# Embedding rows by indirect transfers on GpSimd in place of a one-hot product on TensorE

## The chip, the cores and the metric

The kernel runs on one core of one Trainium2 chip. The time is the device time of one execution in microseconds; the kernel before has a median of 807.42 us in 3 runs (805.93 to 807.51). The profiled execution took 805.65 us; its span, from the first to the last recorded instruction, is 803.5 us.

The engines are TensorE (PE: matmuls; PEld: its weight loads, which overlap them), VectorE (DVE), ScalarE (ACT), GpSimd (POOL) and SyncE (SP, which here issues transfers only). Each runs its own instruction list in order, and they meet through semaphores.

## The reference

Tokens of shape (2, 2048), 0 to 69, become rows of 192 numbers; then one block with a state-space mixer, a gated MLP and a routed mixture of 8 experts follows. Only the embedding is changed:

```
t = minimum(tokens, 63);  color, shape, quantity = t // 16, t % 16 // 4, t % 4
feat_emb = concatenate([color_W[color], shape_W[shape], quantity_W[quantity]])
spec_emb = special_W[clip(tokens - 64, 0, 5)]
emb = where(tokens < 64, feat_emb, spec_emb)
h = emb * sqrt(192) + position                 # (2, 2048, 192)
h = h + block(layernorm(h))                    # the mixer runs along the 2048 tokens
h = h + experts(layernorm(h))                  # 2 of 8 experts per token, and a shared one
```

The host lays the 70 possible rows out in one table (64 combinations of features and 6 special rows), so that a token is the number of its row.

## The kernel before

The 2048 tokens are cut into 16 chunks of 128 (`NC`, `Q`), and a chunk holds both sequences (`NB` = 2), so most tiles are 128 tokens by 2 x 192 numbers, or 128 channels by 256 tokens. The order of every engine's work is written out by hand. Three chunks are under way at a time: `body(p, f, b)` runs the embedding, norm and input products of chunk p, the scan of chunk f = p-1 and the MLP and experts of chunk b = p-2. `ramp` does chunks 0 and 1 up to there, `body` is run 14 times (once written out, 13 times in a loop), and `finale` does the last two chunks.

The embedding of a chunk is `pre`. Before the change it goes: SP fetches the chunk's tokens, broadcast on 70 partitions (`load`, L370), and the position rows; DVE compares them with the row numbers `ids` (`pre_onehot`, L1060), which gives a one-hot tile of 70 x 256; PE multiplies it with the table, which DVE has split into three bf16 parts at the start (`setup_table`, L1002 to L1010), in 6 matmuls (`pre_embed`, L1558); DVE adds the position rows (`pre_add`, L1067) and takes mean and variance (`pre_stats`); POOL raises the variance to the power -0.5 (`rsqrt`, L444); ACT and DVE write the normed rows as high and low halves (L812, L1052), and PE turns them (`pre_turn`, L1572) for the input products.

In a round PE embeds inside `swiglu` (L1864), the gate and up products of chunk b's MLP. These are six pairs (f = 0 to 5) of 10 matmuls on two PSUM banks `p_pair` in turn, so pair f waits until DVE has read pair f-2 (`gt_ready`, L1873; DVE writes `gt` at L1222 from ACT's `sg`, L792). `pre_embed` stands after pair 1, before pair 2. DVE has the one-hot step after `scanned(f, 0)` and `pre_add` after the second `gt` (L1229). POOL has, between `pre(p)` and `norm2(b)` (L603 to L605), nothing.

```
                    if f >= 2:
                        pe.wait_ge(gt_ready, c * NF + f - 1)
                    mlp_gate_up(c, f, p_pair[f % 2])
                    if f == 1 and p is not None:
                        pre_embed(p)
```

Of the kernel before, what the change touches and what calls it, by code (L numbers as in the profile page):

```python
# [21 lines left out]
ALU = mybir.AluOpType  # L22
# [4 lines left out]
BF16 = mybir.dt.bfloat16  # L27
I32 = mybir.dt.int32

NB = 2  # L30
# [70 lines left out]

def program(nc, tokens, position, vocab_ids, table, weights, norms, conv_w, conv_b, shared_rows, d_skip, w_out, w_down,
            w2, identity, lower_ones, triangle_rows, exponent_rows, pair_rows, spread_rows, out):
    with ExitStack() as ctx:
        def sb(name, shape, dt=F32):
            return ctx.enter_context(nc.sbuf_tensor(name, shape, dt))

        def sem(name):
            return ctx.enter_context(nc.semaphore(name))


        ids = sb("ids", [V, 1])
        tab = sb("tab", [V, D])
        tab_rest = sb("tab_rest", [V, 2, D])
        tab3 = sb("tab3", [V, 3, D], BF16)
        w_raw = sb("w_raw", [128, COLS])
# [30 lines left out]

        tok = sb("tok", [V, NB, Q], I32)
        pos = sb("pos", [128, D])
        onehot = sb("onehot", [V, NB, Q], BF16)  # L150
        h0_next = sb("h0_next", [128, NB, D])
# [109 lines left out]
        tokens_in, position_in = sem("tokens_in"), sem("position_in")  # L261
        onehot_ready, emb_done, h0_ready, stat_ready, r0_ready = (sem(n) for n in (
            "onehot_ready", "emb_done", "h0_ready", "stat_ready", "r0_ready"))
        uc_ready, uh_ready, ul_ready, uh_turned, ul_turned, u_hi_ready, u_lo_ready = (sem(n) for n in (
# [76 lines left out]
        def _(sp):  # L341
# [27 lines left out]

            def load(c):  # L370

                if later(c):
                    sp.wait_ge(onehot_ready, c)
                settle(sp)
                sp.dma_start(tok[:], tokens[:, bass.ds(c * Q, Q)].partition_broadcast(V)).then_inc(tokens_in, 16)
                if later(c):
                    sp.wait_ge(h0_ready, c)
                settle(sp)
                sp.dma_start(pos[:], position[bass.ds(c * Q, Q), :]).then_inc(position_in, 16)
# [23 lines left out]
            def body(p, f, b):  # L403
                if p is not None:
                    load(p)
                    sums_in_rows(p)
                if b is not None:
                    store(b)
# [5 lines left out]
            def ramp():  # L414
                load(1)
                load_rows()
                load_columns(slice(COL_G, COL_E), in_mid)
                sums_in_rows(0)
                load_columns(slice(COL_E, COLS), in_experts)
                load_last()  # L420
                sums_in_rows(1)

            sp.dma_start(ids[:], vocab_ids).then_inc(in_first, 16)
            sp.dma_start(tab[:], table).then_inc(in_first, 16)
            load(0)
            sp.dma_start(idf[:], identity).then_inc(in_first, 16)
# [7 lines left out]
        def _(pool):  # L434
            pool.memset(mhalf[:], -0.5).then_inc(setup_p, 1)
            pool.memset(state[:], 0.0).then_inc(setup_p, 1)
            pool.memset(xr[:, :, :, 0:KC - 1], 0.0).then_inc(setup_p, 1)
            pool.memset(ones16[:], 1.0).then_inc(setup_p, 1)
            pool.memset(xd[:], 0.0).then_inc(setup_p, 1)
            pool.memset(bc[0:NS], 0.0).then_inc(setup_p, 1)  # L440
            pool.memset(bt[:, :, 0:NS], 0.0).then_inc(setup_p, 1)
            pool.wait_ge(setup_p, SETUP_P)
# [132 lines left out]

            def ramp():
                keep(0)
                pre(0)
                pre(1)
                steps_decay(0)  # L580
                halo(0)
# [11 lines left out]
            def body(p, f, b):  # L593
# [20 lines left out]
            run(pool, ramp, body, finale)  # L614

        @block.scalar
        def _(act):

            act.wait_ge(in_first, 48)
            act.copy(id16[:], idf[:]).then_inc(setup_a, 1)  # L620
# [365 lines left out]
        def _(ve):  # L986
# [4 lines left out]
            def setup_table():  # L991
# [8 lines left out]
                ve.wait_ge(setup_v, setup_steps.next(0))  # L1000
                ve.wait_ge(in_first, 48)
                ve.tensor_scalar(tab_rest[:, 0, :], tab[:], EMB_SCALE, None, ALU.mult).then_inc(setup_v, 1)  # L1002
                ve.wait_ge(setup_v, setup_steps.next(0))
                ve.tensor_copy(tab3[:, 0, :], tab_rest[:, 0, :]).then_inc(setup_v, 1)
                ve.wait_ge(setup_v, setup_steps.next(0))
                ve.tensor_tensor(tab_rest[:, 1, :], tab_rest[:, 0, :], tab3[:, 0, :], ALU.subtract).then_inc(setup_v, 1)
                ve.wait_ge(setup_v, setup_steps.next(0))
                ve.tensor_copy(tab3[:, 1, :], tab_rest[:, 1, :]).then_inc(setup_v, 1)
                ve.wait_ge(setup_v, setup_steps.next(0))
                ve.tensor_tensor(tab3[:, 2, :], tab_rest[:, 1, :], tab3[:, 1, :], ALU.subtract).then_inc(setup_v, 1)  # L1010
                ve.wait_ge(setup_v, setup_steps.next(0))

# [46 lines left out]

            def pre_onehot(c):  # L1060
                ve.wait_ge(tokens_in, c * 16 + 16)
                if later(c):
                    ve.wait_ge(emb_done, c)
                ve.tensor_scalar(onehot[:], tok[:], float(V - 1), ids[:, 0:1], ALU.min, ALU.is_equal)\
                    .then_inc(onehot_ready, 1)
# [386 lines left out]
            def ramp():  # L1452
                setup_table()
                pre_onehot(0)
                pre_add(0)
                pre_stats(0)
                pre_onehot(1)
# [4 lines left out]
                pre_add(1, p_out[0])  # L1462
                pre_stats(1)
# [35 lines left out]
            def body(p, f, b):  # L1499
# [11 lines left out]
                if p is not None:  # L1511
                    pre_onehot(p)
                swiglu(b, p, f)
# [19 lines left out]
        def _(pe):  # L1533
# [23 lines left out]

            def pre_embed(c, dst=p_misc):  # L1558
                if not later(c):
                    pe.wait_ge(setup_v, SETUP_V)  # L1560
                pe.wait_ge(onehot_ready, c + 1)

                if later(c) and dst is p_misc:
                    pe.wait_ge(s_ready[0], c)
                settle(pe)
                for b in range(NB):
                    for k in range(3):
                        ins = pe.matmul(dst[:, b * D:(b + 1) * D], onehot[:, b, :], tab3[:, k, :],  # L1568
                                        start=(k == 0), stop=(k == 2))
                ins.then_inc(emb_done, 1)  # L1570

            def pre_turn(c, dst=p_misc, low=p_out[1][:, NB * Q:2 * NB * Q]):  # L1572
                if not later(c):
                    pe.wait_ge(setup_a, 1)
                turn(c, dst, low, u_t, uh_ready, ul_ready, uh_turned, ul_turned)

# [287 lines left out]
            def swiglu(c, p, f_):  # L1864
# [6 lines left out]
                for f in range(NF):  # L1871
# [251 lines left out]
N_ROWS = 2  # L2123
SETUP_V = 9
SETUP_P = 7
# [72 lines left out]
```

## Time and profile before

| | us |
|---|---|
| median of 3 runs | 807.42 |
| the profiled execution | 805.65 |
| its span | 803.5 |
| one round of `body` | 47.2 |
| PE busy in the span | 767.3 |
| DVE busy | 643.7 |
| ACT busy | 549.0 |
| POOL busy | 284.5 |

A round repeats every 47.2 us, and inside it PE has hardly a gap. The first 60 us are different: there the weights arrive and are split, the chunks 0 and 1 go through one stage after the other, and PE is busy for 30 to 70% of the time. A row of a timeline gives the start, the duration, engine and line, and in brackets how long the engine sat idle before it and what released it.

### The profile page before, as it was taken

Reading aid. Unit: us, or ns where it says so; the run is one execution under the profiler, and the core shown is the slowest. Engines: PE = TensorE matmul, PEld = TensorE weight load, DVE = VectorE, ACT = ScalarE, POOL = GpSimd, SP = SyncE. Lnnn points to the kernel's source line nnn. Section 1 sums busy time; section 2 is a strip of 40 time slices with the busy share of each in tenths; the row PEclk is TensorE's granted clock in tenths of the full one; section 3 lists DMA queues with packets and bytes.
Section 4 is the critical chain, followed back from the end, with each engine's and each line's share of the span. In section 5 each row is a group of like instructions: output and inputs, shape, how many; then the busy total and the mean of one; then the engine's idle time right before and its main releaser. Section 6 shows DMA issues by size and latency. Waiting matters only on the chain.

```text
span 803.5 us, 23139 instructions
## 1 busy us (share of the span) xinstructions
PE 767.3 (95%) x7374; PEld 655.2 (82%) x7374; DVE 643.7 (80%) x1712; ACT 549.0 (68%) x1228; POOL 284.5 (35%) x427
## 2 busy tenths in 40 slices
PE   3679999999999999999999999999999999999897
PEld 2447888888888888888888888888888888888786
DVE  5699987879788787978878797887889788786745
ACT  4975776767677676767767676776767777676533
POOL 2254342423434242343324234332423433242122
PEclk9899999999999999999999999999999999999999
DMA  7410010000000000000000000000000000000000
GB/s 244 164 66 2 1 26 2 7 19 6 18 0 24 0 6 18 6 18 0 24 0 6 18 3 21 0 21 3 6 18 3 21 0 17 7 6 11 3 1 20
DMA packets 13475, 16.77 MB, mean 21 GB/s; under 512 B 1986, under 2 KB 12104, under 8 KB 13000
## 3 DMA queue, kind: packets, MB, share of 16 engines
q1 hardware_dynamic: 13448, 16.43, 6.4%
q8 instruction: 15, 0.25, 0.1%
q14 instruction: 12, 0.10, 0.0%
HBM read 12.23 MB, written 4.19 MB: 20 GB/s over the span
## 4 chain that ended last, share of the span: by engine, by line
PE 86%; DVE 3%; issue 1%; ACT 1%; POOL 0%; POOLq 0%; DVEq 0%; ACTq 0%
PE bank L1540 39%; PE bank L1932 11%; PE bank L1859 8%; PE bank L1715 5%; PE bank L1704 5%; PE bank L1828 4%; PE bank L1815 3%; PE bank L1806 2%; PE bank L1792 2%; PE bank L1644 1%; DVE mr L1176 1%; PE bank L1568 1%; PE bank L1649 1%; PE bank L1688 1%; PE bank L1899 1%
## 5 line engine op out<-in xcount | busy, mean ns | idle before, releaser
L1176 DVE SCALAR_TENSOR_TENSOR mr<-er,gm 128x512 f32<-128x512 f32 x192 | 126.0, 692 | 5.2 <-ACT er L753 3.5
L753 ACT ACTIVATE er<-bank 128x512 f32<-128x512 f32 x192 | 106.0, 596 | 18.3 <-PE bank L1704 17.7
L1932 PE MATMUL bank<-w2t,w_raw 128*128 128x192 f32 x576 | 112.6, 327 | 0.4 <-DVE w_raw L1345 0.4
L843 ACT ACTIVATE sg<-bank 128x256 f32<-128x256 f32 x144 | 55.1, 383 | 62.3 <-PE bank L1540 51.4
L1115 DVE SCALAR_TENSOR_TENSOR xa<-xr,cw_,xa 128x256 f32<-128x256 f32 x192 | 92.4, 488 | 6.1 <-ACT xa L661 4.5
L1932 PEld LDWEIGHTS bank<-w2t,w_raw 128*128 128x128 f32 x576 | 91.0, 190 | 1.8 <-DVE w_raw L1438 0.7
L792 ACT ACTIVATE sg<-bank 128x256 f32<-128x256 f32 x90 | 34.3, 381 | 65.5 <-PE bank L1540 46.4
L1540 PE MATMUL bank<-x_h,w_hi 128*128 128x256 f16 x288 | 78.6, 273 | 0.0
L1540 PE MATMUL bank<-x_h,wt_lo 128*128 128x256 f16 x288 | 78.7, 273 | 0.0
L1540 PE MATMUL bank<-x_h,w_lo 128*128 128x256 f16 x288 | 78.6, 273 | 0.0
L1540 PE MATMUL bank<-x_l,w_hi 128*128 128x256 f16 x288 | 78.6, 273 | 0.0
L1540 PE MATMUL bank<-x_h,wt_hi 128*128 128x256 f16 x288 | 78.6, 273 | 0.0
L1859 PE MATMUL bank<-wd,gt 128*128 128x192 f32 x384 | 74.2, 329 | 0.4 <-DVE gt L1222 0.4
L1345 DVE TENSOR_TENSOR w_raw<-sg,bank 128x256 f32<-128x256 f32 x144 | 59.9, 416 | 12.2 <-ACT sg L843 11.1
L550 POOL TENSOR_TENSOR w_raw<-w_raw 128x384 f32<-128x384 f32 x64 | 64.0, 1000 | 14.9 <-ACT w_raw L831 8.7
L448 POOL TENSOR_SCALAR var<-mv 128x2 f32<-128x2 f32 x32 | 6.9, 217 | 175.0 <-DVE mv L1253 122.1
L1704 PE MATMUL bank<-ri,lj 128*128 128x512 f16 x192 | 64.3, 383 | 3.6 <-DMA ri<-sums 1.4
L1438 DVE SCALAR_TENSOR_TENSOR w_raw<-bank,cw,w_raw 128x192 f32<-128x192 f32 x128 | 47.5, 413 | 20.4 <-POOL w_raw L550 17.9
L1859 PEld LDWEIGHTS bank<-wd,gt 128*128 128x128 f32 x384 | 60.9, 190 | 1.3 <-DVE gt L1222 0.7
L1715 PE MATMUL bank<-mr,xd 128*32 128x128 f32 x1536 | 56.6, 281 | 2.0 <-DVE mr L1176 1.8
L487 POOL TENSOR_TENSOR state<-state,ends 128x384 f32<-128x384 f32 x31 | 31.4, 1014 | 66.8 <-PE bank L1555 39.9
L1540 PE MATMUL bank<-v_h,w_hi 128*128 128x256 f16 x192 | 52.6, 274 | 1.9 <-DVE gt L1222 1.1
(244 smaller groups left out, 2162.1 us busy)
## 6 DMA issues: line engine op xcount, KB each, us to landing
out<-w_raw SPq DMA_DIRECT2D x16, 192.0 KB, 2.0
pos<-position SPq DMA_DIRECT2D x16, 96.0 KB, 2.9
ri<-exponent_rows SPq DMA_DIRECT2D x1, 1536.0 KB, 6.4
w_raw<-weights SPq DMA_DIRECT2D x1, 1156.0 KB, 5.5
wt_raw<-weights SPq DMA_DIRECT2D x1, 1156.0 KB, 8.8
tok<-tokens SPq DMA_DIRECT2D x16, 70.0 KB
sums<-lj SPq DMA_DIRECT2D x16, 64.0 KB, 1.9
w2t<-w SPq DMA_DIRECT2D x1, 864.0 KB, 11.3
```

The costliest lines, as they stand in the source:

```text
L550: pool.tensor_tensor(acc[:], acc[:], wt_out[:, e % NWT], ALU.add).then_inc(acc_done, 1)
L753: act.activation(er[:, r % NER], p_d[r % 2][:].rearrange("p (h i) -> p h i", h=HG), ACT.Exp)\
L843: act.activation(sg[:, e % 4, :], src[e][:, 0:NB * Q], ACT.Silu).then_inc(sx_ready, 1)
L1115: ve.scalar_tensor_tensor(xa[:, m], xr[:, m, :, k:k + Q], cw_[:, m, k:k + 1], xa[:, m], ALU.mult, ALU.add)\
L1176: ve.scalar_tensor_tensor(mr[:, r % NMR], er[:, r % NER], 1.0, gm[:, r // NQ, :].unsqueeze(1).to_broadcast([128, HG, Q]), ALU.min, ALU.mult)\
L1345: ve.tensor_tensor(hh[:, e % NHH, :], sg[:, e % 4, :], src[e][:, NB * Q:2 * NB * Q], ALU.mult)\
L1438: ins = ve.scalar_tensor_tensor(acc[:, b], p_ex[e][:, b * D:(b + 1) * D], cw[:, b, e - 1:e], acc[:, b], ALU.mult, ALU.add)
L1540: ins = pe.matmul(out_, a, b, start=(i == 0), stop=(i == len(parts) - 1))
L1704: pe.matmul(p_d[r % 2][:].rearrange("p (h i) -> p h i", h=HG), lj[:, b, f, :], ri[:, of, b, f, :], start=True, stop=True).then_inc(d_done, 1)
L1715: ins = pe.matmul(p_y[row:row + 32, k * Q:(k + 1) * Q], xd[:, b, h, :], mr[:, r % NMR, heads.index(h), :], start=False, stop=(h % 2 == 1), ...
L1859: ins = pe.matmul(dst[:, b * D:(b + 1) * D], gt[:, f, b * Q:(b + 1) * Q], wd[:, f, :], start=(f == 0 and b == 0), stop=(f == NF - 1), skip ...
L1932: ins = pe.matmul(p_ex[e][:, b * D:(b + 1) * D], hh[:, e % NHH, b * Q:(b + 1) * Q], w2t[:, e, :], start=True, stop=True)
```

## The change

The table stays in DRAM. The tokens come in as one number per partition and sequence (128 x 2) and not broadcast. POOL clips them into row numbers and issues two indirect transfers, one per sequence, each of which fetches 128 rows of 192 numbers from the table into the new tile `emb`. POOL does so for chunk p+1 in the round in which chunk p is embedded; SP fetches the tokens of p+1 ahead of that. DVE scales `emb` and adds the position in one instruction with three operands. The one-hot step, the splitting of the table on DVE and the 6 matmuls go. `pre_turn` takes over the wait that `pre_embed` had for its bank. At the start POOL issues the first two transfers ahead of its memsets.

```
-            def load(c):
-                if later(c):
-                    sp.wait_ge(onehot_ready, c)
+            def load_tokens(c):
+                if later(c):
+                    sp.wait_ge(row_ready, c)
                 settle(sp)
-                sp.dma_start(tok[:], tokens[:, bass.ds(c * Q, Q)].partition_broadcast(V)).then_inc(tokens_in, 16)
+                sp.dma_start(tok[:], tokens[bass.ds(c * Q, Q), :]).then_inc(tokens_in, 16)
+
+            def load_position(c):
...
             def body(p, f, b):
                 if p is not None:
-                    load(p)
+                    load_tokens(p + 1)
+                    load_position(p)
...
             def ramp():
-                load(1)
+                load_tokens(1)
+                load_position(1)
                 load_rows()
                 load_columns(slice(COL_G, COL_E), in_mid)
+                load_tokens(2)
                 sums_in_rows(0)
...
-            sp.dma_start(ids[:], vocab_ids).then_inc(in_first, 16)
-            sp.dma_start(tab[:], table).then_inc(in_first, 16)
-            load(0)
+            load_tokens(0)
+            load_position(0)
...
+            def embed(c):
+                pool.wait_ge(tokens_in, c * 16 + 16)
+                if later(c):
+                    pool.wait_ge(emb_in, c * 32)
+                settle(pool)
+                pool.tensor_scalar(row[:], tok[:], float(V - 1), 0.0, ALU.min, ALU.max).then_inc(row_ready, 1)
+                pool.wait_ge(row_ready, c + 1)
+                if later(c):
+                    pool.wait_ge(h0_ready, c)
+                settle(pool)
+                for b in range(NB):
+                    pool.indirect_dma_start(emb[:, b, :], None, table, bass.IndirectOffsetOnAxis(row[:, b:b + 1], 0))\
+                        .then_inc(emb_in, 16)
...
             def ramp():
+                embed(0)
+                pool.memset(state[:], 0.0).then_inc(setup_p, 1)
...
                 keep(0)
                 pre(0)
+                embed(1)
                 pre(1)
+                embed(2)
                 steps_decay(0)
...
                 if p is not None:
                     pre(p)
+                    embed(p + 1)
                 norm2(b)
...
+            pool.wait_ge(emb_in, 32 * (NC + 1))
...
-            def pre_add(c, src=p_misc):
-                ve.wait_ge(emb_done, c + 1)
+            def pre_add(c):
+                ve.wait_ge(emb_in, c * 32 + 32)
                 ve.wait_ge(position_in, c * 16 + 16)
                 if later(c):
                     ve.wait_ge(h0_copied, c)
-                ve.tensor_tensor(h0_next[:], src[:, 0:NB * D].rearrange("p (b d) -> p b d", b=NB),
-                                 pos[:].unsqueeze(1).to_broadcast([128, NB, D]), ALU.add).then_inc(h0_ready, 1)
+                ve.scalar_tensor_tensor(h0_next[:], emb[:], EMB_SCALE, pos[:].unsqueeze(1).to_broadcast([128, NB, D]),
+                                        ALU.mult, ALU.add).then_inc(h0_ready, 1)
...
-                    if f == 1 and p is not None:
-                        pre_embed(p)
...
             def ramp():
-                pe.wait_ge(in_first, 48)
-                pre_embed(0)
+                pe.wait_ge(in_first, 16)
                 pre_turn(0, p_misc, p_pair[1][:, 0:NB * Q])
-                pre_embed(1, p_out[0])
```

PE in the loop's `swiglu`, between the last product of pair 1 and the first of pair 2 (`v_h`, `v_l` are the high and low halves of the MLP's input). Before:

```order
L1540 MATMUL bank<-v_h,w_lo 128x256
L1540 MATMUL bank<-v_h,wt_lo 128x256
L1561 REGISTER_ALU
L1568 MATMUL bank<-tab,onehot 128x192 x6
L1873 ISA
L1540 MATMUL bank<-v_h,w_hi 128x256
```

The same place with the change:

```order
L1540 MATMUL bank<-v_h,w_lo 128x256
L1540 MATMUL bank<-v_h,wt_lo 128x256
L1862 ISA
L1540 MATMUL bank<-v_h,w_hi 128x256
```

The six matmuls are gone, and the wait for `gt` (the ISA row) follows the last product of pair 1 at once.

POOL in the ramp, before (`h` is the copy of the embedded rows, `r` the result of the power, `dt_` the first step of the decays of chunk 0):

```order
L462 COPY h<-h_next 128x384
L448 ISA
L448 TENSOR_SCALAR var<-mv 128x2
L450 TENSOR_TENSOR r<-var,mhalf 128x2
L448 TENSOR_SCALAR var<-mv 128x2
L450 TENSOR_TENSOR r<-var,mhalf 128x2
L516 TENSOR_TENSOR dt_<-am_,dl 128x48
```

With the change:

```order
L471 COPY h<-h_next 128x384
L443 TENSOR_SCALAR var<-mv 128x2
L445 TENSOR_TENSOR r<-var,mhalf 128x2
L452 TENSOR_SCALAR row<-tok 128x2
L458 DMA emb<-table,row 128x192 x2
L443 TENSOR_SCALAR var<-mv 128x2
L445 TENSOR_TENSOR r<-var,mhalf 128x2
L452 TENSOR_SCALAR row<-tok 128x2
L458 DMA emb<-table,row 128x192 x2
L525 TENSOR_TENSOR dt_<-am_,dl 128x48
```

Two pairs of transfers now stand between the powers of chunk 0 and 1 and ahead of the decays of chunk 0.

SP in the ramp, with the change, around the tokens of chunk 2:

```order
L356 DMA ri<-exponent_rows 128x6144
L357 DMA lj<-pair_rows 64x512
L360 DMA w_raw<-weights 128x1536
L361 DMA wt_raw<-weights 128x1536
L373 DMA tok<-tokens 128x2
L388 DMA sums<-lj 64x512
```

Before, no tokens stood there; those of chunk 2 were fetched in the first round.

## Rows read from the trace of the kernel before

**Rows 1.** Page, part 1: busy time and share of the span per engine.
```profile
PE 767.3 (95%) x7374; PEld 655.2 (82%) x7374; DVE 643.7 (80%) x1712; ACT 549.0 (68%) x1228; POOL 284.5 (35%) x427
```

**Rows 2.** Busy time in one round: PE, PEld, DVE, ACT, POOL; then L1568 alone.
```profile
398.60:445.80 47.20, 47.13 (x464) 40.60 (x462) 39.09 (x107) 33.75 (x78) 17.25 (x27) 1.00 0.04 10
...
398.60:445.80 47.20, 0.66 (x6) 0.53 (x6) 1.00 0.04 10
```

**Rows 3.** Timeline of a round around the embedding matmuls.
```profile
404.80 0.37 ACT L792 ACTIVATE sg<-bank 128x256 f32<-128x256 f32 x1
...
405.15 0.66 PE L1568 MATMUL bank<-tab,onehot 70*128 70x192 bf16 x6
405.19 0.42 DVE L1222 TENSOR_TENSOR gt<-sg,bank 128x256 f32<-128x256 f32 x1 [0.96 <-ACT sg L792]
...
405.67 0.10 PEld L1540 LDWEIGHTS bank<-v_h,w_hi 128*128 128x128 f16 x1
```

**Rows 4.** Timeline of the same round, DVE's embedding steps and pair 4 of the MLP.
```profile
403.89 0.34 DVE L1064 TENSOR_SCALAR onehot<-tok,ids 70x256 bf16<-70x256 int32 x1
...
406.46 0.55 DVE L1072 TENSOR_TENSOR h_next<-bank,pos 128x384 f32<-128x384 f32 x1
...
408.64 0.91 DVE L1222 TENSOR_TENSOR gt<-sg,bank 128x256 f32<-128x256 f32 x2
...
409.11 0.10 PEld L1540 LDWEIGHTS bank<-v_h,w_hi 128*128 128x128 f16 x1
```

**Rows 5.** Groups of instructions of one round: three-operand instructions of DVE (busy us, mean ns).
```profile
L1176 DVE SCALAR_TENSOR_TENSOR mr<-er,gm 128x512 f32<-128x512 f32 x13 | 8.5, 686 | 0.1
...
L1115 DVE SCALAR_TENSOR_TENSOR xa<-xr,cw_,xa 128x256 f32<-128x256 f32 x12 | 5.7, 480 | 0.4 <-ACT xa L661 0.3
```

**Rows 6.** Timeline of POOL in the same round.
```profile
408.63 0.70 POOL L450 TENSOR_TENSOR r<-var,mhalf 128x2 f32<-128x2 f32 x1
416.53 0.23 POOL L448 TENSOR_SCALAR var<-mv 128x2 f32<-128x2 f32 x1 [7.20 <-DVE mv L1253]
```

**Rows 7.** POOL line L476 in all rounds: ns min/median/max.
```profile
L476 POOL TENSOR_TENSOR xw<-xd,ends x31: 837/839/2350, 31.3 to 724.0; 128x384 f32<-128x384 f32 x31
```

**Rows 8.** Position rows, 16 transfers: issue to landing.
```profile
DMA to landing us min/median/max: 2.1/2.9/3.4
```

**Rows 9.** Timeline of the start.
```profile
0.73 0.46 SPq L423 DMA_DIRECT2D ids<-vocab_ids  x1
...
9.02 0.56 DVE L1072 TENSOR_TENSOR h_next<-bank,pos 128x384 f32<-128x384 f32 x1 [1.41 <-PE bank L1568]
...
11.24 0.70 POOL L450 TENSOR_TENSOR r<-var,mhalf 128x2 f32<-128x2 f32 x1
...
15.46 0.56 DVE L1072 TENSOR_TENSOR h_next<-bank,pos 128x384 f32<-128x384 f32 x1 [0.25 <-PE bank L1568]
...
18.17 0.21 DVE L1132 TENSOR_TENSOR dx<-bank,shared 128x48 f32<-128x48 f32 x1 [0.43 <-PE bank L1540]
18.41 0.21 DVE L1135 SCALAR_TENSOR_TENSOR dn<-dx 128x48 f32<-128x48 f32 x1
...
19.45 0.23 ACT L698 ACTIVATE de<-dn 128x48 f32<-128x48 f32 x1
```

**Rows 10.** Timeline of the start: weights, decays of chunk 0 and what follows them.
```profile
11.68 0.54 SPq L363 DMA_DIRECT2D wt_raw<-weights  x1
...
21.31 0.29 POOL L516 TENSOR_TENSOR dt_<-am_,dl 128x48 f32<-128x48 f32 x1 [2.96 <-ACT dl L704]
...
25.46 0.18 PE L1676 MATMUL bank<-pb,triangles 128*128 128x48 f16 x1
...
26.08 0.72 ACT L720 CAST lj<-bank 32x256 f16<-32x256 f32 x2
...
27.60 0.63 ACT L687 ACTIVATE xs<-xa 128x512 f32<-128x512 f32 x1 [0.27 <-DVE xa L1115]
```

**Rows 11.** Page, part 6: transfer of L363 (KB, us to landing).
```profile
wt_raw<-weights SPq DMA_DIRECT2D x1, 768.0 KB, 9.2
```

More of the change, by code:

```diff
@@ L28 @@
 I32 = mybir.dt.int32
+U32 = mybir.dt.uint32
 NB = 2
@@ L99, in reached, with program @@
         return c * self.per + self.n
-def program(nc, tokens, position, vocab_ids, table, weights, norms, conv_w, conv_b, shared_rows, d_skip, w_out, w_down,
+def program(nc, tokens, position, table, weights, norms, conv_w, conv_b, shared_rows, d_skip, w_out, w_down,
             w2, identity, lower_ones, triangle_rows, exponent_rows, pair_rows, spread_rows, out):
@@ L109, in sem @@
             return ctx.enter_context(nc.semaphore(name))
[L112 to L115, printed above, removed]
         w_raw = sb("w_raw", [128, COLS])
@@ L145, in program @@
         mhalf = sb("mhalf", [128, 2])
-        tok = sb("tok", [V, NB, Q], I32)
+        tok = sb("tok", [128, NB], I32)
+        row = sb("row", [128, NB], U32)
+        emb = sb("emb", [128, NB, D])
         pos = sb("pos", [128, D])
-        onehot = sb("onehot", [V, NB, Q], BF16)
         h0_next = sb("h0_next", [128, NB, D])
@@ L261, in program @@
         tokens_in, position_in = sem("tokens_in"), sem("position_in")
-        onehot_ready, emb_done, h0_ready, stat_ready, r0_ready = (sem(n) for n in (
-            "onehot_ready", "emb_done", "h0_ready", "stat_ready", "r0_ready"))
+        row_ready, emb_in, h0_ready, stat_ready, r0_ready = (sem(n) for n in (
+            "row_ready", "emb_in", "h0_ready", "stat_ready", "r0_ready"))
         uc_ready, uh_ready, ul_ready, uh_turned, ul_turned, u_hi_ready, u_lo_ready = (sem(n) for n in (
@@ L435, in _ @@
             pool.memset(mhalf[:], -0.5).then_inc(setup_p, 1)
[L436 to L442, printed above, removed]
             def rsqrt(c, ready, src, scale, bias, mid, dst, chain, steps, k, done):
@@ L576, in ramp @@
             def ramp():
+                embed(0)
+                pool.memset(state[:], 0.0).then_inc(setup_p, 1)
+                pool.memset(xr[:, :, :, 0:KC - 1], 0.0).then_inc(setup_p, 1)
+                pool.memset(ones16[:], 1.0).then_inc(setup_p, 1)
+                pool.memset(xd[:], 0.0).then_inc(setup_p, 1)
+                pool.memset(bc[0:NS], 0.0).then_inc(setup_p, 1)
+                pool.memset(bt[:, :, 0:NS], 0.0).then_inc(setup_p, 1)
+                pool.wait_ge(setup_p, SETUP_P)
                 keep(0)
                 pre(0)
+                embed(1)
                 pre(1)
+                embed(2)
                 steps_decay(0)
@@ L614, in _ @@
             run(pool, ramp, body, finale)
+            pool.wait_ge(emb_in, 32 * (NC + 1))
         @block.scalar
         def _(act):
-            act.wait_ge(in_first, 48)
+            act.wait_ge(in_first, 16)
             act.copy(id16[:], idf[:]).then_inc(setup_a, 1)
@@ L1000, in setup_table @@
                 ve.wait_ge(setup_v, setup_steps.next(0))
[L1001 to L1011, printed above, removed]
             def setup_first():
@@ L1058, in low_in @@
                 ve.tensor_copy(lo[:], src).then_inc(ready, 1)
-            def pre_onehot(c):
-                ve.wait_ge(tokens_in, c * 16 + 16)
-                if later(c):
-                    ve.wait_ge(emb_done, c)
-                ve.tensor_scalar(onehot[:], tok[:], float(V - 1), ids[:, 0:1], ALU.min, ALU.is_equal)\
-                    .then_inc(onehot_ready, 1)
-            def pre_add(c, src=p_misc):
-                ve.wait_ge(emb_done, c + 1)
+            def pre_add(c):
+                ve.wait_ge(emb_in, c * 32 + 32)
                 ve.wait_ge(position_in, c * 16 + 16)
@@ L1453, in ramp @@
                 setup_table()
-                pre_onehot(0)
                 pre_add(0)
                 pre_stats(0)
-                pre_onehot(1)
                 setup_first()
@@ L1461, in ramp @@
                 pre_split(0, p_pair[1][:, 0:NB * Q])
-                pre_add(1, p_out[0])
+                pre_add(1)
                 pre_stats(1)
@@ L1510, in body @@
                     scanned(f, 0)
-                if p is not None:
-                    pre_onehot(p)
                 swiglu(b, p, f)
@@ L1556, in turn @@
                 ins.then_inc(low_turned, 1)
[L1558 to L1570, printed above, removed]
             def pre_turn(c, dst=p_misc, low=p_out[1][:, NB * Q:2 * NB * Q]):
@@ L1574, in pre_turn @@
                     pe.wait_ge(setup_a, 1)
+                    pe.wait_ge(setup_v, SETUP_V)
+                elif dst is p_misc:
+                    pe.wait_ge(s_ready[0], c)
                 turn(c, dst, low, u_t, uh_ready, ul_ready, uh_turned, ul_turned)
@@ L2123 @@
 N_ROWS = 2
-SETUP_V = 9
+SETUP_V = 4
 SETUP_P = 7
@@ L2173 @@
     arrays = {
-        "tokens": x, "position": position, "vocab_ids": np.arange(V, dtype=f32)[:, None],
+        "tokens": np.concatenate([np.transpose(x), np.zeros((Q, NB), np.int32)], axis=0), "position": position,
         "table": np.concatenate([features, L0_tok_special_W], axis=0),
```

## The prediction, made before the changed kernel was run

> **What bounds the kernel now.** I read the page's busy times first, then a table of stretches over whole rounds, then the timeline of one round at the place that the change touches, and last the timeline of the start. The reader is to see four things. PE is busy for 767.3 of 803.5 us [rows 1], and in a round of 47.20 us for 47.13 [rows 2]: by the average PE is the bound, and whatever leaves it is a gain. But an engine can be called busy and still be held, if the work given to it just fills a wait. So the second thing is what ends last at the start of pair 2 of the MLP. There ACT, behind the load of a table, writes the first `sg` from 404.80, DVE makes the first `gt` of it from 405.19 to 405.61 after an idle 0.96, and PE begins pair 2, which needs that `gt`, at 405.67 [rows 3]. The embedding matmuls start at 405.15 and their last ends its streaming at about 405.64 (the row's 0.66 holds the pipeline's tail). Both arrive together, within 0.05 us. Third, POOL, which gets the transfers, waits 7.20 us between the power of chunk p and that of chunk b [rows 6]. Fourth, the start is a chain of single steps through all engines, without cover.
>
> **The matmuls that go.** 6 matmuls with 0.66 us in each of the 14 rounds [rows 2]; the piece of PE's time that they fill is 405.15 to 405.67, 0.52 us, so 14 x 0.52 = 7.3 us if PE were the bound there. Without them PE stands at pair 2 at 405.15 and finds `gt` missing until 405.61. The chain that makes `gt` (ACT's exponentials, its table load, `sg`, DVE) has neither the one-hot step nor the embedding in it. The hop from DVE's end to PE's start is 0.06 now and stays. I take the gain as 0 per round, at most 0.03. The later waits of PE hang on `gt` too, so nothing moves ahead behind this point. DVE's one-hot of 0.34 us goes as well, and lies in front of DVE's idle 0.96 [rows 3, 4]: 0.
>
> **The add that changes form.** `pre_add` took 0.55 us [rows 4] with one operand in PSUM. Now it is a three-operand instruction over 384 numbers with both in SBUF. The nearest rows are 480 ns for 256 numbers and 686 for 512 [rows 5]; in between lies 583, and at about one number per ns above 256 it would be 610. So it is 0.03 to 0.06 longer; I take 0.05. This falls on the one stretch of DVE that PE waits for next: DVE runs from 405.19 to the third `gt` with nearly no idle time, that `gt` ends at 409.06 (the first half of 0.91 from 408.64), and PE loads the weights of pair 4 at 409.11, right behind it [rows 4]. There is no slack, so 14 x 0.05 = +0.7 us. The bounds are 0 (if PE still has those 50 ns) and 14 x 0.08 = 1.1.
>
> **The transfers in a round.** On POOL, behind the power that ends at 409.33: a clip of 0.23 (as the small tensor_scalar in [rows 6]) with a hop of 0.1, and two transfers. The trace has no such instruction. From below, an issue on SP takes 0.46 [rows 9]; from above, POOL's slowest pass over 128 partitions takes 2.35, its usual one 0.84 [rows 7]. I take 1.0 each, near the usual pass, since every one of 128 rows has to be handled. That makes 2.3 us in a hole of 7.20, nothing. It decides only from 3.4 us each. The tokens have a whole round to land, and so have the rows. Also nothing.
>
> **The start.** Now the tokens go first, at 0.73 [rows 9], and land like the position rows after 2.9 [rows 8], at 3.6. Clip and hop give 3.95, two transfers 5.95, landing again 2.9: the add can start at 8.85, where now it starts at 9.02 [rows 9]. So the table and one-hot work that goes (five steps on DVE, one compare, a product) is paid back by two trips through memory. The power of chunk 0 ends 2.92 after the add (11.94 against 9.02), so at 11.8. Then POOL takes chunk 1: 12.1, two transfers to 14.1, and a landing amid the weights, for which I take the slowest of the position rows, 3.4; the bounds are 2.1 and the 9.2 that the big weight transfer took [rows 8, 11]. The second add starts at 17.5, against 15.46 [rows 9]. Behind it on DVE stand the statistics and `steps_dt`: the add to the end of `dn` took 3.16, of which 0.43 was a wait for PE. That gives 20.2 for ACT's exponential, which now starts at 19.45 [rows 9]: +0.8.
> The third pair stands ahead of the decays of chunk 0. Its tokens are issued by SP behind the second piece of the weights, which is issued at 11.68 and lands 9.2 later, at 20.9 [rows 10, 11]; on the same queue the tokens should not be sooner. 20.9 + 0.33 + 2.0 = 23.2, where the decays start at 21.31 now [rows 10]: a new wait of 1.9 on POOL. The sums on PE end at 25.64 now and would end at 27.5; ACT needs them at 26.08 + 0.8 = 26.9, so `lj` is 1.45 late, and at ACT's next step, which has 0.27 of wait to give, 1.2 is left [rows 10]. The two delays lie over each other: +1.2 us for the start. With 0.46 and 2.1 for the unknown terms the add of chunk 0 is 1.9 earlier and the start gains 0.2 to 0.8; with 2.35 and 3.4 the second add alone comes 5.9 later than in my sum, and the start costs 7.
>
> The page "DMA: Bandwidth & Descriptors" of the Trainium skill (section "Anatomy of one DMA — SWDGE (gpsimd) path") has such a transfer at about 2.0 us plus its bytes by 436 GB/s, 2.2 for 96 KB. The same-sized position rows took 2.9 in this trace, so I stay with the row; by the page the second add would come at 15.6, and the start would cost only what the tokens of chunk 2 cost, some +1.
>
> **The sum.** 0 for the matmuls and the transfers in a round, 0.7 for the add, 1.2 for the start: +1.9 on the profiled execution's 805.65 (803.5 of span and 2.15 around it), 807.5. The median of the runs lies 1.77 above that execution, so I forecast 807.42 + 1.9 = 809.3 us.
>
> **Rivals.**
> (a) The saved PE time comes through: 14 x 0.52 = -7.3, with the same losses 802.0 us. For it: PE is 95% busy [rows 1]. Against it: `gt` ends 0.06 before pair 2 begins [rows 3]. It decides if PE can start pair 2 before 405.61, or if ACT's table load comes earlier in the new rhythm.
> (b) The start gains: transfers of 0.5 us each that land in 2.1, and tokens of chunk 2 that do not queue behind the weights. Start -0.8, rounds +0.4: 807.0. For it: SP's issues are that short. Against: POOL's rows.
> (c) The transfers are slow, 2 to 3.4 us each, but the hole in the round hides them. Only the start pays, four of them in line on the way to the second add: +5 to +11 in all, 813 to 819.
> (d) While POOL writes out a pair of transfers, DVE cannot use two operands from SBUF. Here 409.4 to 411.8 holds the low half of `u_t`, a mask and a `gt`; if DVE stands until POOL is done, it loses up to 1.2 us, of which PE, 0.7 ahead of need, sees 0.6 to 1.2: 14 x 0.9 = +12, 822 us. What speaks for it: the same pass of POOL takes 0.84 or, beside a long DVE instruction, 2.35 [rows 7], so the two do block each other. Against: POOL's work here is on addresses, and reads 128 numbers. In "SBUF — State Buffer" of the Trainium skill, section "Who interferes with whom", the two share a pair of ports that one instruction holds as a whole, and DVE's instructions with two SBUF operands are named; the 2.35 agrees, and for a transfer no run here shows it.
> (e) Over 3.4 us each: POOL is late for the norm of chunk b. At 4 us, 14 x 1.2 and a start of +12: 837 us.
>
> **Chances.** My forecast 0.54 (its own range 807.6 to 811.5); (a) 0.07; (b) 0.12; (c) 0.14; (d) 0.10; (e) 0.03. A measurement of this kernel tells 0.2%, 1.6 us, from no change: 805.8 to 809.0. Faster: (a) and a little of (b), 0.09. Within: most of (b) and the lower part of my range, 0.36. Slower: the rest, 0.55. The range leaves out (a), the far half of (c), (d) and (e): 805.6 to 815.
>
> **What would show it.** Right: pair 2 still starts 0.06 behind the first `gt`, and PE shows an idle 0.5 us there, ended by DVE's `gt`, with a round of 47.2 to 47.25 us; PE busy falls by some 8 us with no gain. The new add takes 0.58 to 0.61. In the start POOL waits for the tokens of chunk 2 until about 21, and the second add starts near 17.5. Wrong: a round of 46.7 (rival a); DVE's `u_t` or mask at 410 to 412 stretched (rival d); POOL's transfers over 1.6 us each or POOL's 7.20 us gone; the first round starting no later than now.

## The result, and the profile after

| | before | after |
|---|---|---|
| median of 5 runs, us | 807.26 | 810.69 |
| lowest to highest | 805.93 to 807.51 | 809.61 to 811.66 |
| profiled execution | 805.65 | 809.61 |
| its span | 803.5 | 807.8 |
| PE busy | 767.3 | 760.4 |
| start of the first `hm` | 69.76 | 74.22 |
| start of the 15th `hm` | 732.14 | 736.61 |

The ratio is 1.0052, with an interval of 1.0041 to 1.0063: slower by half a per cent. 809.3 was forecast, 810.69 measured.

`hm` is DVE's sum of `h` and the mixer's output; it stands once in every round. Its two rows divide the loss. From the first to the 15th it is 662.38 us before and 662.39 after: the rounds cost nothing and give nothing. All 4.46 us are lost before the first `hm`. The end, from the 15th `hm` on, is 0.2 shorter, and what lies around the span is 0.34 shorter, hence +3.96 for the profiled execution.

First the page of the kernel after, its busy times (against [rows 1]):

```profile
PE 760.4 (94%) x7278; PEld 646.7 (80%) x7278; DVE 638.0 (79%) x1691; ACT 548.5 (68%) x1228; POOL 327.3 (41%) x478
```

PE lost 6.9 us of work, POOL gained 42.8. Where PE's time went stands in the timeline of a steady round, at the place of [rows 3]:

```profile
409.54 0.42 DVE L1226 TENSOR_TENSOR gt<-sg,bank 128x256 f32<-128x256 f32 x1 [1.22 <-ACT sg L814]
...
410.01 0.10 PEld L1540 LDWEIGHTS bank<-v_h,w_hi 128*128 128x128 f16 x1 [0.64 <-DVE gt L1226]
410.02 0.28 PE L1540 MATMUL bank<-v_h,w_hi 128*128 128x256 f16 x1 [0.36 <-DVE gt L1226]
...
410.81 0.55 DVE L1076 SCALAR_TENSOR_TENSOR h_next<-emb,pos 128x384 f32<-128x384 f32 x1
```

`gt` ends at 409.96 and pair 2 begins 0.05 behind it, as before. In front of it PE now stands where it multiplied by the one-hot tile. DVE waits 1.22 instead of 0.96, because its one-hot step is gone too. The groups of instructions say the same over all rounds (busy us, mean ns, then the idle time before the group and what ended it). Before:

```profile
L1540 PE MATMUL bank<-v_h,w_hi 128*128 128x256 f16 x192 | 52.6, 274 | 1.9 <-DVE gt L1222 1.1 <-issue 0.8
```

After:

```profile
L1540 PE MATMUL bank<-v_h,w_hi 128*128 128x256 f16 x192 | 52.7, 274 | 6.9 <-DVE gt L1226 6.2 <-issue 0.8
```

The wait for `gt` grew by 5.1 us over the kernel, 0.36 in each of the 14 rounds; the rest of the 0.52 that the matmuls filled is covered by the tail of the product in front. POOL in the same round, against [rows 6]:

```profile
412.98 0.69 POOL L445 TENSOR_TENSOR r<-var,mhalf 128x2 f32<-128x2 f32 x1
413.64 0.20 POOL L452 TENSOR_SCALAR row<-tok 128x2 uint32<-128x2 int32 x1
414.71 1.11 POOL L458 DMA_INDIRECT emb<-table,row  x1 [0.88 <-POOL row L452]
416.12 0.97 POOL L458 DMA_INDIRECT emb<-table,row  x1 [0.30 <-issue]
420.87 0.23 POOL L443 TENSOR_SCALAR var<-mv 128x2 f32<-128x2 f32 x1 [3.79 <-DVE mv L1257]
```

A pair of transfers holds POOL from 413.84 to 417.09, and of the 7.20 us of idle time 3.79 are left. The line of the transfers, in all rounds:

```profile
L458 POOL DMA_INDIRECT emb<-table,row x34: 952/1098/2939, 4.0 to 699.3; - x34
...
DMA to landing us min/median/max: 2.5/2.8/6.7
```

The start (the times of before are in [rows 9, 10]):

```profile
2.83 0.18 POOL L452 TENSOR_SCALAR row<-tok 128x2 uint32<-128x2 int32 x1 [2.00 <-DMA tok<-tokens]
...
3.98 1.21 POOL L458 DMA_INDIRECT emb<-table,row  x1 [0.97 <-POOL row L452]
...
5.50 0.96 POOL L458 DMA_INDIRECT emb<-table,row  x1 [0.31 <-issue]
...
8.83 0.56 DVE L1076 SCALAR_TENSOR_TENSOR h_next<-emb,pos 128x384 f32<-128x384 f32 x1 [6.93 <-DMA emb<-table,row]
...
11.72 0.51 POOL L452 TENSOR_SCALAR row<-tok 128x2 uint32<-128x2 int32 x1
13.08 1.13 POOL L458 DMA_INDIRECT emb<-table,row  x1 [0.85 <-POOL row L452]
14.52 0.97 POOL L458 DMA_INDIRECT emb<-table,row  x1 [0.30 <-issue]
...
20.51 0.56 DVE L1076 SCALAR_TENSOR_TENSOR h_next<-emb,pos 128x384 f32<-128x384 f32 x1 [5.53 <-DMA emb<-table,row]
...
23.16 0.24 ACT L720 ACTIVATE de<-dn 128x48 f32<-128x48 f32 x1 [3.88 <-DVE dn L1139]
23.40 0.27 POOL L452 TENSOR_SCALAR row<-tok 128x2 uint32<-128x2 int32 x1
...
26.88 0.43 POOL L525 TENSOR_TENSOR dt_<-am_,dl 128x48 f32<-128x48 f32 x1
...
32.10 0.73 ACT L742 CAST lj<-bank 32x256 f16<-32x256 f32 x2 [2.06 <-PE bank L1665]
```

The first add comes at 8.83, 0.19 before the old one. The second comes at 20.51 where it was 15.46, +5.05, and it waits for its rows. The delay then runs down the chain: ACT's exponential +3.7 (19.45 to 23.16), the decays +5.57 (21.31 to 26.88, with the third pair of transfers ahead of them), `lj` +6.0 (26.08 to 32.10). Of this 1.6 is made good by the first `hm`. `lj` is what ACT makes of the sums of the decays, for PE to build the masks of the scan with.

What lay beside the second pair is in the transfers of 12 to 18 us (KB, us to landing):

```profile
wt_raw<-weights SPq DMA_DIRECT2D x1, 768.0 KB, 9.4
emb<-table,row POOLq DMA_INDIRECT x2, 6.3
tok<-tokens SPq DMA_DIRECT2D x1, 1.0 KB, 8.8
```

### The profile page after: what moved, and what is told of

The parts are those of the page before. It is cut to its first block, busy times and chain, and to the rows that moved or that the text cites. A ratio compares the mean times of both kernels' runs of the same rounds, so it can differ in the third digit from the quotient of the medians.

```text
span 807.8 us, 23032 instructions
## 1 busy us (share of the span) xinstructions
PE 760.4 (94%) x7278; PEld 646.7 (80%) x7278; DVE 638.0 (79%) x1691; ACT 548.5 (68%) x1228; POOL 327.3 (41%) x478
## 4 chain that ended last, share of the span: by engine, by line
PE 80%; ACT 4%; issue 4%; DVE 3%; POOL 0%; ACTq 0%; DVEq 0%; POOLq 0%
PE bank L1540 36%; PE bank L1919 11%; PE bank L1848 8%; PE bank L1704 5%; PE bank L1693 4%; PE bank L1817 4%; PE bank L1804 3%; PE bank L1795 2%; PE bank L1781 2%; ACT er L775 2%; PE bank L1633 1%; ACT L995 1%; DVE gt L1226 1%; PE bank L1638 1%; PE bank L1677 1%
```

## Experiments

Eight kernels ran, 4 to 11 executions each, and 15 or 21 executions of the kernel before beside them, on the same chip; its medians there were 806.06 to 806.28. Times of different rows are compared by their ratios, since the chips differ. "First `hm`" is where the first round's `hm` starts, "round" the distance of two `hm` in the steady rounds.

| kernel | median us | ratio to before | first `hm` | round |
|---|---|---|---|---|
| before | | | 69.76 | 47.16 |
| after | 810.69 | 1.0052 (1.0041 to 1.0063) | 74.22 | 47.19 |
| weights wait for the rows | 815.03 | 1.0110 (1.0095 to 1.0126) | 79.58 | 47.19 |
| the same, tokens of chunk 2 ahead | 807.25 | 1.0013 (1.0004 to 1.0023) | 70.99 | 47.20 |
| decays of chunk 0 first | 808.67 | 1.0035 (1.0021 to 1.0049) | 73.35 | 47.20 |
| before, 2 of 6 matmuls | 803.95 | 0.9976 (0.9967 to 0.9985) | 69.59 | 47.15 |
| before, 12 for 6 matmuls | 811.78 | 1.0066 (1.0052 to 1.0080) | 70.24 | 47.62 |
| chunk 1 fetched at once | 804.97 | 0.9981 (0.9970 to 0.9991) | 69.87 | 47.19 |
| the same, wait filled | 805.35 | 0.9988 (0.9975 to 1.0001) | 70.13 | 47.19 |
| wait filled, turn moved | 815.38 | 1.0118 (1.0096 to 1.0140) | 68.75 | 47.84 |

### Who makes the second add late

```
             def ramp():
                 load_tokens(1)
                 load_position(1)
+                sp.wait_ge(emb_in, 64)
+                settle(sp)
                 load_rows()
```

> The changed kernel, but SP issues the rows, the second piece of the weights and the tokens of chunk 2 only when the gathered rows of chunk 1 have landed. Theory: those rows land 6 us after their issue because their packets share the 16 DMA engines with the weights; alone they land in about 2.8, so the second add on DVE starts near 17.4 instead of 20.5 and the time falls by about 3 us, from 810.7 to about 807.7, although the weights come some 7 us later. Rival: the late landing is made on GpSimd or by DVE's weight splitting beside it (1.17 us instructions with two operands in SBUF), which this run leaves in place: then the second add stays at 20.5 and the time at 810.7 or above.

Measured: 815.03. The timeline of this kernel's start:

```profile
17.41 0.56 DVE L1078 SCALAR_TENSOR_TENSOR h_next<-emb,pos 128x384 f32<-128x384 f32 x1 [2.01 <-DMA emb<-table,row]
...
28.75 0.19 POOL L454 TENSOR_SCALAR row<-tok 128x2 uint32<-128x2 int32 x1 [8.46 <-DMA tok<-tokens]
...
36.51 0.74 ACT L744 CAST lj<-bank 32x256 f16<-32x256 f32 x2 [9.69 <-PE bank L1667]
```

With no weights on their way the second add starts at 17.41, 3.10 earlier: the traffic beside the rows is what made it late. DVE's weight splitting, the rival, still stands beside the transfers (1.17 us from 13.90). But the kernel got slower, where 807.7 was forecast. The tokens of chunk 2 stand behind the weights on SP's queue, and now POOL reaches them first and waits 8.46 us for 1 KB, with the decays of chunk 0 behind it. In the kernel after these tokens were issued at 12.32 and landed at about 21.1, 2.3 us before POOL came for them; here they are issued at 19.64 only, so most of the 8.46 is made by this edit. That this wait, and not the later weights, cost the time was a reading of the trace only, so it got a run of its own:

```
                 load_position(1)
+                sp.wait_ge(emb_in, 64)
+                load_tokens(2)
                 load_rows()
                 load_columns(slice(COL_G, COL_E), in_mid)
-                load_tokens(2)
```

> The kernel after, with SP waiting for the gathers of chunk 1 before it issues the weight transfers, as in the run that came to 815.03, but with the tokens of chunk 2 (1 KB) issued right behind that wait and ahead of the weights. It tells apart two reasons for that run's loss against the kernel after (first round 5.4 us later). Theory: the second add was then at 17.41 as wanted, and the whole loss came from the 1 KB of tokens behind the weights, which held GpSimd for 8.46 us. Then the third row step comes at about 20.4 in place of 28.75, the decays start at 23.6 to 24.0 in place of 32.14, the casts lj on ScalarE at 28 to 29 (32.10 in the kernel after), and the first round starts 6 to 8 us earlier than the 79.58 of that run, at 71.5 to 73.5, before the 74.22 of the kernel after; rounds 47.19; the time 807 to 809.5. Rival: the weights themselves, 5 us later, are what the start waits for; then the first round stays at 77 to 79.6 and the time at 812 to 815, with PE or ScalarE released by a weight transfer.

Measured: 807.25, within the 807 to 809.5 of the theory. Its start:

```profile
17.18 0.56 DVE L1077 SCALAR_TENSOR_TENSOR h_next<-emb,pos 128x384 f32<-128x384 f32 x1 [2.20 <-DMA emb<-table,row]
...
20.06 0.27 POOL L453 TENSOR_SCALAR row<-tok 128x2 uint32<-128x2 int32 x1
...
23.55 0.40 POOL L526 TENSOR_TENSOR dt_<-am_,dl 128x48 f32<-128x48 f32 x1
...
28.76 0.74 ACT L743 CAST lj<-bank 32x256 f16<-32x256 f32 x2 [2.17 <-PE bank L1666]
```

All four rows lie near what was expected, and the first `hm` comes at 70.99, somewhat better than the 71.5 to 73.5 expected. Moving a 1 KB transfer ahead of the weights is worth 8.59 us here (79.58 to 70.99); that the weights come later costs nothing that the start shows. Against the kernel after, the undisturbed second pair gives 3.23 us.

### The third pair ahead of the decays

```
                 pre(1)
-                embed(2)
                 steps_decay(0)
+                embed(2)
```

> The changed kernel, but GpSimd does the decays of chunk 0 before the gathers of chunk 2. Theory: the decays start near 25.0 instead of 26.9, but most of what they were late is made good a few us later, where TensorE no longer waits at its lower clock; the time falls by 0.3 to 1.0 us, to about 810.0. Rival 1: the pair of gathers ahead of the decays costs its full 2.1 us: 808.6. Rival 2: it costs nothing, since the second add is late anyway: 810.7.

```profile
25.72 0.28 POOL L525 TENSOR_TENSOR dt_<-am_,dl 128x48 f32<-128x48 f32 x1 [1.64 <-ACT dl L726]
...
30.49 0.72 ACT L742 CAST lj<-bank 32x256 f16<-32x256 f32 x2
```

The decays start 1.16 earlier than in the kernel after, although the second add of this execution was 0.68 later, at 21.19. `lj` gains 1.61 and the first `hm` 0.87. The median, 808.67, is the figure of rival 1, but this chip ran the kernel before at 806.06: the loss against it is 2.6 us, for the 3.4 of the kernel after, so 0.8 is gained, as the theory had it. The third pair does cost about a microsecond, but through POOL's time (23.40 to 26.86 in the kernel after), not through the tokens, which had landed by then.

### What the matmuls were worth

The kernel before, with 2 of its 6 embedding matmuls in every chunk (the low parts of the table are left out), and with its 6 done twice in the rounds:

```
-                    for k in range(3):
+                    for k in range(1):
```

> The kernel before with 2 instead of 6 embedding matmuls per chunk (only the first bf16 part of the table is used, so the embedding is coarser). Theory: TensorE then reaches pair 2 of the MLP some 0.35 us earlier and waits for gt; time unchanged, 807.3 within 0.4. Rival: TensorE's busy time is the bound: 14 x 0.35 less, 802.4.

```
+                for _ in range(2 if dst is p_misc and later(c) else 1):
                     for b in range(NB):
                         for k in range(3):
```

> The kernel before with the 6 embedding matmuls of a round done twice (the same result written again). Theory: the wait for gt is just filled by the first six, so the second six cost their full time, 14 x 0.50 = 7.0 us: 814.3. Rival: the wait still has room, or another engine sets the round: clearly less than 814, in the extreme 807.3.

PE's wait for `gt` is 1.1 us in the kernel before, in three places outside the steady rounds. With 2 matmuls it is:

```profile
L1540 PE MATMUL bank<-v_h,w_hi 128*128 128x256 f16 x192 | 52.7, 274 | 4.5 <-DVE gt L1222 3.7 <-issue 0.8
```

With none (the kernel after) it is 6.2, so the work taken out comes back as wait, and the round stays at 47.15 to 47.19. With 12 the round is 47.62, 0.46 longer, of the 0.52 that six more matmuls take; between medians it is 5.7 us for the 7.0 forecast. The six filled a wait up to some 0.06 us: more is paid, less shortens no round. The median with 2 matmuls does not fit that fully, nor its forecast of an unchanged time: at 803.95 it is 2.1 us under that of the kernel before, 806.06. Its trace, of an execution of 805.26, shows equal rounds and a first `hm` only 0.17 earlier. The other runs lie in two groups, 803.64 to 803.95 and 804.65 to 805.93, and only one of the upper was profiled. What the lower group did differently stays open; the kernel before, too, ran between 803.90 and 807.93 on one of the chips. The 2.1 are less than half of the 14 x 0.35 = 4.9 that PE's time would have given.

### Chunk 1 fetched at once

The kernel after, with tiles of their own for the tokens, row numbers and rows of chunk 1. All four transfers of chunks 0 and 1 stand at POOL's start, the long memsets behind the first norm, and the third pair behind the decays:

```
             def ramp():
-                embed(0)
...
+                embed(0)
+                embed(1)
                 keep(0)
                 pre(0)
-                embed(1)
+                pool.memset(state[:], 0.0).then_inc(setup_p, 1)
...
                 pre(1)
-                embed(2)
                 steps_decay(0)
                 halo(0)
                 weighted_x(0, 0)
                 weighted_x(0, 1)
+                embed(2)
```

> The changed kernel with another start: the tokens of chunk 1 are fetched right behind those of chunk 0 into tiles of their own, GpSimd issues the four gathers of chunks 0 and 1 back to back, before the big pieces of the weights are on the queues, three of its memsets come behind the power of chunk 0, and the gathers of chunk 2 stand behind the weighted inputs of chunk 0, some 10 us later. The rounds are those of the changed kernel. Theory: the whole loss lies in the start and both of its causes are gone, so the second add comes near 12 to 14 and no longer sets anything; the time is that of the kernel before within 1 us, 806 on this chip. Rival: the gathers cost something in every round (slower DVE or GpSimd, or the transfers of a round): then 1 to 3 us over the kernel before remain.

```profile
3.98 1.21 POOL L474 DMA_INDIRECT emb<-table,row  x1 [0.97 <-POOL row L468]
5.50 0.97 POOL L474 DMA_INDIRECT emb<-table,row  x1 [0.30 <-issue]
...
6.97 0.98 POOL L460 DMA_INDIRECT emb<-table,row  x1 [0.27 <-POOL row L457]
8.25 0.96 POOL L460 DMA_INDIRECT emb<-table,row  x1 [0.30 <-issue]
...
15.45 0.55 DVE L1097 SCALAR_TENSOR_TENSOR h_next<-emb,pos 128x384 f32<-128x384 f32 x1
...
21.59 0.29 POOL L541 TENSOR_TENSOR dt_<-am_,dl 128x48 f32<-128x48 f32 x1 [3.29 <-ACT dl L743]
```

The second add is back at 15.45. The 12 to 14 of the forecast was missed, but it waits for no transfer any more: it follows at once on DVE's own work, the splitting of the weights and the low half of `u` (to 15.53). The decays start 0.28 after those of before, the first `hm` 0.11. 4.35 of the 4.46 us are recovered: the start held the whole loss. At 804.97 this is 0.19% under the kernel before, with an interval wholly below 1. The profiled executions don't show it: their spans are 803.7 and 803.5. Part of it lies outside the span: in every run of every kernel with indirect transfers 1.76 to 1.85 us lie around it, in those without 2.12 to 2.25. Why, no run tells, nor where the rest of the 1.3 us between the medians comes from.

The gap in front of a pair is 0.27 for chunk 1 and 0.97 for chunk 0. The code of chunk 1 lacks one step between the row numbers and the transfer, `settle`, which raises a semaphore. That this step makes the longer gap is likely, but no run took it out alone.

### Filling the wait

Four products with `skip` of the second sequence, moved from later in the round to the place of the embedding matmuls:

```
-                pe.wait_ge(y_sum[0], c + 1)
-                for k in range(KT):
+                for k in range(2, KT):
                     skipped_x(1, k)
...
                     mlp_gate_up(c, f, p_pair[f % 2])
+                    if f == 1 and f_ is not None:
+                        pe.wait_ge(y_sum[0], f_ + 1)
+                        skipped_x(1, 0)
+                        skipped_x(1, 1)
```

> e5_early, and two of the three skip products of sequence 1 (0.49 us on TensorE) move from behind the state products to the place where the embedding matmuls stood, ahead of pair 2 of the MLP. Theory: they fill the wait for gt, but TensorE then comes 0.49 us sooner to the transposes of the normed rows (turn_x), which start at 418.69 in the kernel before, 0.03 behind VectorE; so the wait moves there and little is gained: within 1.5 us of e5_early. Rival: TensorE has that room, and 14 x 0.49 = 6.9 us are gained, 799.

The groups of PE in this kernel, and then the timeline:

```profile
L1561 PE MATMUL bank<-v_h,w_hi 128*128 128x256 f16 x192 | 52.6, 274 | 1.6 <-DVE gt L1247 0.8 <-issue 0.8
...
L1561 PE MATMUL bank<-u_h,w_hi 128*128 128x256 f16 x112 | 31.1, 278 | 5.8 <-ACT er L792 4.8 <-DVE u_l L1086 1.0
```

```profile
405.69 0.61 PE L1801 MATMUL bank<-xs,skip 128*128 128x128 f32 x4
...
417.06 0.27 PE L1561 MATMUL bank<-u_h,w_hi 128*128 128x256 f16 x1 [0.34 <-ACT er L792]
```

The wait for `gt` is filled in the rounds (the 0.8 left are two waits outside them), and the round is 47.19 as ever. The time is 805.35 against 804.97: little is gained, as the theory said, but the wait did not go where it said. Where the products were taken away, ahead of the input products and not at the turn of the normed rows, PE now waits. The profile names ACT's exponentials `er`, which the masks are made of: 4.8 us over the kernel, where the same group waited 1.0, for `u_l` alone, with the products in place. PE's gap moved to the next thing that PE waits for. For one more step the turn of the router's input (`turned`), which stood behind the input products, was put behind two of the masked products:

```
+                masked(c, (6, 7))
                 turned()
-                masked(c, range(NQ, NR))
+                masked(c, range(8, NR))
```

> e8_fill, and the transposes of the normed rows stand behind the products of masks 6 and 7 (0.49 us) in place of ahead of them. Theory: both waits are then filled and the 0.5 us of a round that the embedding matmuls took are really saved, 14 x 0.45 = 6.3 us: about 800. Rival: a third wait behind them (router, or the pair 4 that starts 0.05 behind its gt) takes it: 805 or more.

```profile
423.58 0.37 ACT L672 CAST x_h<-bank 128x256 f16<-128x256 f32 x1 [1.51 <-PE bank L1912]
...
424.45 0.42 DVE L1073 TENSOR_TENSOR x_l<-bank,x_h 128x256 f16<-128x256 f32 x1 [0.56 <-ACT x_h L673]
...
425.67 0.10 PEld L1561 LDWEIGHTS bank<-w_hi,x_h 128*128 128x128 f16 x1 [0.87 <-issue]
```

That theory fell: 815.38, 0.65 a round slower. The casts of `x_h` on ACT now wait 1.51 for the turn (0.79 with the turn in its place), DVE's `x_l` waits for them, and PE stands 0.87 in front of the router's first product (0.49). In this kernel the turn has to come early: moved behind 0.49 us of products it costs 0.65, so the chain from it to the router, through ACT and DVE, has no slack of that size. The wait for `er` was still there (0.34). Which chain sets the 47.2 was not settled: PE waited by turns in front of pair 2, of the input products and of the router, and each place filled opened another.

## Why the prediction came out as it did

**The matmuls, 0: right.** Pair 2's start 0.05 behind `gt`, the longer idle times in front of it and PE busy 6.9 lower (some 8 foreseen) are what the prediction named. The wait for `gt` holds 5.1 of it. The kernels with 2 and 12 matmuls show it from both sides, up to the open 2.1 us of the first.

**The add, +0.7: wrong, it is 0.** The new instruction takes 0.550 to 0.557 us, the old one 0.55 to 0.56. The bound of 0 was the right end. The two rows of [rows 5], 480 ns for 256 numbers and 686 for 512, were not a line on which 384 lies.

**Transfers in a round, 0: right,** with 0.95 to 1.1 us each for the estimated 1.0. Left out were the gaps, 0.88 ahead of the first and 0.30 between the two, so that clip and pair hold POOL for 3.4 us (413.67 to 417.09) instead of 2.3. The 3.79 of idle time left cover that. The rounds are 0.03 us longer in most places; against it stands the first round, 0.34 shorter. Why, no run tells.

**Rival (d), DVE held by POOL's transfers: refuted.** Between 413.84 and 417.09 DVE's low half of `u_t` took 0.77 and its mask 0.68 (0.77 and 0.69 before). The Trainium skill, in "SBUF — State Buffer", section "Who interferes with whom", names DVE's instructions with two SBUF operands beside a GpSimd instruction that reads SBUF as those that hold each other up; DVE lost nothing beside these transfers. The other way round the record has something that neither the prediction nor the rounds show. In the first round of every kernel with indirect transfers the pair took 2.94 and 1.81, beside DVE's subtraction of the last weights, which has both operands in SBUF:

```profile
84.49 2.94 POOL L458 DMA_INDIRECT emb<-table,row  x1 [0.86 <-POOL row L452]
85.09 1.35 DVE L1049 TENSOR_TENSOR wt_lo<-wt_raw,wt_hi 128x1156 f16<-128x1156 f32 x1
87.73 1.81 POOL L458 DMA_INDIRECT emb<-table,row  x1 [0.30 <-issue]
```

The subtraction takes 1.35 in the kernel before as well, so if the two held each other up, it was POOL that stood. In the start a pair beside DVE's three-operand splitting (1.17 us from 13.48) took its usual 1.13 and 0.97, and no run tells the reason for the difference. It cost nothing: the first round is the one that got shorter.

**The start, +1.2: the term that was mis-sized.** The prediction counts a landing from the end of the pair on POOL, so that is how it is checked here. For chunk 0 it had the pair's end at 5.95 and 2.9 for the landing, 8.85; measured were 6.46 and 2.37, 8.83. That the sum came out to 0.02 is luck: the gaps left out and a landing too long cancelled. For chunk 1 it had 14.1 and 3.4, 17.5; measured were 15.49 and 5.02, 20.51. So the step that failed has two parts. One is the hold of POOL: clip and pair from 11.72 to 15.49 are 3.8 us for 2.3, because of the gaps of 0.85 and 0.30 and a clip of 0.51, which makes 1.4 of the 3.0 us. The other is the landing "amid the weights, for which I take the slowest of the position rows, 3.4", with 5.0 (6.0 to 6.7 from the start of each transfer), which makes 1.6. In both runs without weights beside it the add came at 17.41 and 17.18, close to the forecast 17.5, but by the same luck: the pair ended at 15.9 and 15.5 and landed in 1.5 and 1.7. The position rows were the wrong row for "amid the weights", since the slowest of those took 3.4 while [rows 11] had 9.2 for a transfer of the same stretch. By the page "DMA: Bandwidth & Descriptors" of the Trainium skill, section "Anatomy of one DMA — SWDGE (gpsimd) path", the landing would be an estimated 2.2; the median of 2.8 from the start of a transfer is near it, but the 6.3 in that stretch is not, and the measurement decides.

**The tokens of chunk 2: right in time, not what was waited for.** They took 8.8 us for 1 KB and landed at about 21.1 (20.9 forecast), but POOL reached them only at 23.40, since the second add was later still. So the sign "POOL waits for the tokens of chunk 2 until about 21" did not come. The prediction had the tokens set the decays, at 23.2, with the add's smaller delay hidden under theirs; in the run the add set them, and they started at 26.88.

**In sum:** +4.46 in the start for +1.2, 0 in the rounds for +0.7, -0.2 at the end and -0.34 around the span, which were not foreseen: +3.96 for the profiled execution and +3.43 between medians, against +1.9. The forecast's median stood 1.77 above the profiled execution, the measured one stands 1.08 above it, and that is luck too. The side, the bounding place and the range held; the start was 3.3 us too short, and the add, the part around the span and the medians gave back more than half of that. Rival (c)'s +5 to +11 would be 812 to 818 and not 813 to 819; nothing hangs on it.

## What to carry to other kernels

Work that just fills an engine's wait for another engine may cost nothing: here taking 6 matmuls out shortened no steady round, though PE was busy for 47.13 of 47.20 us. Adding as much again shows in one run how full the wait is. A transfer that a start-up chain waits for belongs ahead of the bulk transfers, in the order of its queue and in time: here the rows took 6.3 us beside the weights and 2.8 elsewhere, and a 1 KB transfer behind them 8.8, for 1.7 elsewhere. Fetch what the second step needs together with the first, into buffers of its own: that recovered 4.35 of the 4.46 us. And a forecast that counts an instruction's duration must count the gaps beside it, here 1.2 us for a pair of transfers of 2.1.

## What the runs showed of the hardware

An indirect transfer of 128 rows of 768 bytes held GpSimd for 0.95 to 1.2 us as a rule (2.94 and 1.81 in the first round), with a gap of 0.84 to 0.97 behind the instruction that made the row numbers (0.27 in one place) and 0.30 between two. It landed 2.8 us after its start (median), and 6.0 to 6.7 beside 768 KB and 1536 KB transfers on another queue, with the DMA engines 97% busy.

In the start PE's granted clock fell after idle stretches. The kernel before from 36 to 40, then the kernel after, by stretches (PE, PEld, DVE, ACT, POOL busy, then clock, DMA share, GB/s):

```profile
36.00:40.00 4.00, 4.00 (x36) 2.94 (x39) 2.39 (x5) 2.73 (x7) 0.70 (x1) 0.60 1.00 408
```

```profile
12.00:18.00 6.00, 3.74 (x28) 2.51 (x29) 2.35 (x5) 2.59 (x7) 2.33 (x3) 1.00 0.97 387
...
24.00:30.00 6.00, 0.98 (x6) 0.48 (x6) 4.64 (x12) 5.92 (x11) 4.37 (x9) 0.65 0.14 33
30.00:36.00 6.00, 4.76 (x39) 4.23 (x40) 3.46 (x10) 3.71 (x8) 1.15 (x3) 0.50 0.04 11
36.00:40.00 4.00, 2.89 (x21) 1.81 (x20) 0.77 (x2) 3.92 (x10) 1.63 (x2) 0.99 0.62 188
```

From 24 to 30 PE had 0.98 us of work, and from 30 to 36 it worked at 0.50, the lower of its two levels (1.2 GHz). From 36 on it had the full one, where the kernel before had 0.60 in the same stretch. That is where part of the delay was made good: the six products of `xs` with the state took 1.65 us from 37.50 before, and 0.94 from 42.64 after, 0.7 of the 1.6. So the delay in the start did not carry through one to one.
